# Attention with a product-key expert layer: the filter's statistics, gates and norms reordered against the residual addition

## The reference

```python
xn = layernorm(x)
# attention: 16 heads of 8
q = xn @ Wq + bq;  latent = xn @ Wl + bl            # latent: 32
k = latent @ Wk + bk;  v = latent @ Wv + bv
attn = softmax(q @ k.T * 8 ** -0.5) @ v @ Wo + bo
# expert layer: 8 heads of 32
f = (xn @ fWq + fbq).reshape(B, S, 8, 32)
f = (f - f.mean((0, 1, 2))) / sqrt(f.var((0, 1, 2)) + 1e-5) * gamma + beta   # over all tokens
f0, f1 = l2norm(f[..., :16]), l2norm(f[..., 16:])
s0, s1 = f0 @ l2norm(key0).T, f1 @ l2norm(key1).T    # 32 keys each
# the best 4 of s0 and of s1, softmax over their 16 sums -> weights w of 16 experts
out = x + attn + sum_k w_k * gelu(down[idx_k] . xn) * up[idx_k]
```

## Time and profile before

| | |
|---|---|
| runs | 390.57, 387.48, 390.49 us; median 390.49 |
| profiled execution | 391.01 us, its span 389.2 us |
| TensorE busy | 327.7 us (84%), weight loads 175.9 |
| VectorE busy | 339.8 us (87%) |
| ScalarE busy | 261.1 us (67%) |
| GpSimd busy | 254.7 us (65%) |
| mean granted TensorE clock | 0.956 |
| DMA | 24.81 MB, mean 64 GB/s |

### The profile page before, as it was taken

The page is one execution under the profiler, slowest core; times in us unless marked ns, Lnnn a source line. Parts: engine busy times, 40 slices in busy tenths (PEclk is TensorE's granted clock), DMA queues, the critical chain, the costliest instruction groups (busy, mean ns, idle before and its releaser), DMA issues.

```text
span 389.2 us, 9689 instructions
## 1 busy us (share of the span) xinstructions
PE 327.7 (84%) x3080; PEld 175.9 (45%) x3080; DVE 339.8 (87%) x1409; ACT 261.1 (67%) x412; POOL 254.7 (65%) x544
## 2 busy tenths in 40 slices
PE   3999960878699889898989889898989898898975
PEld 2455540433235445444545445444545454454443
DVE  5699989767977999999999999999999999999571
ACT  4689960697755676676676776666676766767771
POOL 6488899000665676857767676758667677758780
PEclk9999995599659999999999999999999999999999
DMA  5565664000944041231404051432404050000100
GB/s 165 143 185 149 176 179 120 2 1 7 114 49 81 24 62 41 60 77 22 99 2 98 16 84 43 56 70 31 92 7 98 9 92 18 2 17 3 29 15 13
DMA packets 45886, 24.81 MB, mean 64 GB/s; under 512 B 5452, under 2 KB 45708, under 8 KB 45836
## 3 DMA queue, kind: packets, MB, share of 16 engines
q1 hardware_dynamic: 45836, 24.20, 29.1%
HBM read 15.54 MB, written 8.39 MB: 61 GB/s over the span
## 4 chain that ended last, share of the span: by engine, by line
PE 52%; DVE 26%; ACT 11%; issue 7%; POOL 3%; POOLq 0%; ACTq 0%; DVEq 0%
PE bank L605 12%; DVE negm L822 9%; PE bank L634 8%; PE bank L651 8%; PE SI L531 6%; DVE r_sb L886 6%; PE SJ L584 6%; ACT Eb L363 3%; DVE bnv L785 3%; ACT s_sb L380 2%; PE bank L676 2%; PE bank L678 2%; PE bank L677 2%; DVE fst L744 1%; PE SI L456 1%
## 5 line engine op out<-in xcount | busy, mean ns | idle before, releaser
L822 DVE TENSOR_REDUCE negm<-SI 128x4 f32<-128x1024 f32 x128 | 154.8, 1219 | 5.5 <-PE SI L531 5.1
L413 ACT ACTIVATE Eb<-SJ 128x1024 f32<-128x1024 f32 x128 | 130.4, 1019 | 32.1 <-PE SJ L584 31.9
L1039 POOL TENSOR_TENSOR prod<-r_sb,a 128x1024 f32<-128x1024 f32 x31 | 60.2, 1943 | 26.9 <-issue 25.9
L605 PE MATMUL bank<-Eb,vhat 128*18 128x256 f32 x1024 | 70.3, 393 | 0.0
L531 PE MATMUL SI<-KS,QS 48*128 48x256 bf16 x512 | 52.0, 282 | 14.2 <-DVE negm L822 13.9
L584 PE MATMUL SJ<-QS,KS 50*128 50x256 bf16 x512 | 51.7, 282 | 9.0 <-ACT Eb L413 8.8
L866 DVE MAX8 top<-s_sb 128x8 f32<-128x32 f32 x512 | 50.6, 181 | 4.6 <-ACT s_sb L380 4.5
L886 DVE MATCH_REPLACE8 r_sb<-top,s_sb 128x36 f32<-128x36 f32 x256 | 43.1, 181 | 0.0
L531 PEld LDWEIGHTS SI<-KS,QS 48*128 48x128 bf16 x512 | 18.2, 96 | 53.0 <-issue 46.7
L651 PE MATMUL bank<-cst,prod 128*128 128x128 f32 x256 | 34.6, 278 | 4.2 <-ACT s_sb L380 3.7
L634 PE MATMUL bank<-kblk,fqT 128*128 128x256 f32 x128 | 37.1, 413 | 0.5 <-ACT s_sb L380 0.4
(11 more groups left out here) (145 smaller groups left out, 615.9 us busy)
## 6 DMA issues: line engine op xcount, KB each, us to landing
qk_parts<-parts SPq DMA_DIRECT2D x48, 128.0 KB, 2.4
QS<-qk_parts SPq DMA_DIRECT2D x32, 96.0 KB
KS<-qk_parts SPq DMA_DIRECT2D x32, 96.0 KB
x_sb<-L_attn_x SPq DMA_DIRECT2D x8, 256.0 KB, 3.9
QS<-qk_parts SPq DMA_DIRECT2D x32, 64.0 KB
KS<-qk_parts SPq DMA_DIRECT2D x32, 64.0 KB
out<-ysb SPq DMA_DIRECT2D x16, 128.0 KB, 3.1
QS<-qk_parts SPq DMA_DIRECT2D x32, 32.0 KB
```

What stands on the lines that cost most here:

```text
L413: A(Eb[:, n % 4, :], SJ[:, :], ACT.Exp).then_inc(s["ex"], 1)
L605: last = mm(psO[32 * c:32 * c + 2 * VC, (q % 2) * S:(q % 2 + 1) * S], vhat[:, v0:v0 + 2 * VC], Eb[:, (2 * g + c // 2) % 4, e0:e0 + S], sta ...
L822: V.tensor_reduce(negm[:, bb % 2, :, :, pr].rearrange("p t e -> p e t"), SI[slot % 2][:, :].rearrange("p (e t j) -> p e t j", e=2, j=S), a ...
L1039: TT(prod[:, t, :, :, :], r_sb[:, hs, 0:NK].unsqueeze(2).to_broadcast([P, FH, TOP, NK]), a0[:, hs, :].unsqueeze(3).to_broadcast([P, FH, TO ...
```

## The change

- `fbq` is added when ScalarE evacuates the features (`features`), so the addition to the mean (L785), two `bnv` columns and the second offset go. The two `fbq` loads move from the third group of loads to the second (`WLOADS`, semaphore `w`), ahead of six loads of `x`.
- With one offset for both halves, the squares of a chunk are one instruction of 1,024 columns, one chunk a slot in slots 2 to 9, and the scaling in place is one instruction a batch.
- The last chunk's round stands by itself: TensorE makes features, then q and k, then v; ScalarE evacuates the features ahead of the q and k parts; VectorE takes the statistics first and weaves q, k and v between the steps to the scale. ScalarE's second parts of the last chunk come after the first square.
- `downT` is evacuated by ScalarE. In each slot TensorE makes the scores `si` first, then norms, then the gate; gates are in slots 0 to 7, norms in 2 to 9. The key product is in slot 3, its mask on VectorE in slot 4; inverses in slots 4, 6, 8, 10; root in slot 10, transpose and copy in slot 11.
- The residual addition waits for `bn`.

```diff
-        sq = [Eb[:, 1 + i, :].rearrange("p (r n) -> p r n", r=2) for i in range(2)]
+        sq = [Eb[:, 1 - i, :].rearrange("p (r n) -> p r n", r=2) for i in range(2)]
...
-                A(fqT[:, r, c * CH:(c + 1) * CH], psF[i % 3], ACT.Copy).then_inc(s["f_ev"], 1)
+                A(fqT[:, r, c * CH:(c + 1) * CH], psF[i % 3], ACT.Identity, bias=vecs[:, 4 + r:5 + r]).then_inc(s["f_ev"], 1)
...
+            features(NC - 1, 0)
+            features(NC - 1, 1)
+            first_part(NC - 1, 0)
+            first_part(NC - 1, 1)
+            act.wait_ge(s["dT"], 1)
+            A(downT[:, :], psX[1][:, 0:E], ACT.Copy).then_inc(s["downT"], 1)
+            act.wait_ge(s["bc"], 1)
+            A(bnv[:, 6:7], bnv[:, 5:6], ACT.Sqrt).then_inc(s["bd"], 1)
...
+                    A(sq[c % 2], fqT[:, :, c * CH:(c + 1) * CH], ACT.Square,
+                      bias=bnv[:, 8:9], scale=bnv[:, 7:8]).then_inc(s["sq"], 1)
+                    if c == 0:
+                        second_part(NC - 1, 0)
+                        second_part(NC - 1, 1)
...
+            for c in range(NC - 1):
+                project_qk(c)
+                project_f(c)
+                turn_x(c + 1)
+                project_v(c)
+            pe.wait_ge(s["xnT"], NC)
+            project_f(NC - 1)
+            project_qk(NC - 1)
+            project_v(NC - 1)
+            bn_mean()
+            pe.wait_ge(s["w2"], NW2)
+            mm(psX[1][:, 0:E], down_sb[:, :], ident, start=True, stop=True).then_inc(s["dT"], 1)
...
+                if FILTER <= slot < FILTER + NC:
+                    norms(slot - FILTER)
+                c = slot
+                if c < NC:
...
+                    mm(psG[c % 2], downT[:, :], xnT[:, c * CH:(c + 1) * CH], start=True, stop=True).then_inc(s["g"], 1)
+                if slot == 3:
+                    pe.wait_ge(s["krep"], 1)
+                    mm(psM[:, 0:NK], keys_rep[:, :, :, :].rearrange("k h a d -> k (h a d)"), cst[0:NK, 0:NK],
+                       start=True, stop=True).then_inc(s["kmm"], 1)
...
+            feature_moments(NC - 2)
             feature_moments(NC - 1)
+            dve.wait_ge(s["f_st"], 2 * NC)
+            for r in range(2):
+                last = V.bn_aggr(fmv[:, r, :], fst[:, r, :, :])
+            last.then_inc(s["ba"], 1)
+            q_ev(NC - 1)
+            bn_shift()
+            k_ev(NC - 1)
+            bn_deviation()
+            v_rows(NC - 1)
+            bn_scale()
...
-            V.tensor_tensor(bnv[:, 0:2], fmv[:, :, 0], vecs[:, 4:6], ALU.add).then_inc(s["ba"], 1)
...
                     if slot == 4:
-                        pool.wait_ge(s["xn"], NC)
+                        pool.wait_ge(s["bn"], 1)
```

More of the change, by code:

```diff
@@ L332, in _ @@
             deviations(1)
-            for c in range(NC):
-                if c + 1 < NC:
-                    normalise(c + 1)
+            for c in range(NC - 1):
+                normalise(c + 1)
                 first_part(c, 0)
@@ L346, in _ @@
                     A(keys_n[:, :, 1], keys_n[:, :, 0], ACT.Sqrt).then_inc(s["kn3"], 1)
+            features(NC - 1, 0)
[6 more added lines that the diff above has]
+            A(bnv[:, 6:7], bnv[:, 5:6], ACT.Sqrt).then_inc(s["bd"], 1)
             for slot in range(NSLOT):
                 k = slot % 8
[L350 to L365, removed]
                 if FILTER <= slot < FILTER + NC:
                     c = slot - FILTER
+                    if c == 0:
+                        act.wait_ge(s["bn"], 1)
+                        act.wait_ge(s["xT"], NC)
+                    if c >= 2:
+                        act.wait_ge(s["n2"], c - 1)
+                    A(sq[c % 2], fqT[:, :, c * CH:(c + 1) * CH], ACT.Square,
+                      bias=bnv[:, 8:9], scale=bnv[:, 7:8]).then_inc(s["sq"], 1)
+                    if c == 0:
+                        second_part(NC - 1, 0)
+                        second_part(NC - 1, 1)
                     act.wait_ge(s["g"], c + 1)
@@ L420, in _ @@
                 if k == 6 and slot < NPAIR * B:
[L422 to L426, removed]
+                    fb = fqT[:, :, slot // 8 * S:(slot // 8 + 1) * S]
+                    A(fb, fb, ACT.Identity, bias=bnv[:, 8:9], scale=bnv[:, 7:8]).then_inc(s["ff"], 1)
+                if slot == FILTER + NC:
                     act.wait_ge(s["n2r"], NC // 2)
@@ L486, in _ @@
             pe.wait_ge(s["wkv_ev"], 1)
[L487 to L499, removed]
             def bn_mean():
                 pe.wait_ge(s["ba"], 1)
-                pe.wait_ge(s["downT"], 1)
                 for r in range(2):
-                    last = mm(psX[0][:, 0:1], avg, bnv[:, r:r + 1], start=(r == 0), stop=(r == 1))
+                    last = mm(psX[0][:, 0:1], avg, fmv[:, r, 0:1], start=(r == 0), stop=(r == 1))
                 last.then_inc(s["ba"], 1)
@@ L552, in _ @@
                 if slot == 0:
-                    bn_mean()
-                if slot == 1:
                     bn_variance()
[L556 to L564, removed]
+                if slot == FILTER + NC + 1:
                     pe.wait_ge(s["n2s"], 1)
@@ L626, in _ @@
                     t = k - 1
+                    if b == 0 and t == 0:
+                        pe.wait_ge(s["kblk"], 1)
                     if t == 0:
@@ L750, in _, with bn_shift, bn_deviation, bn_scale @@
             scales(1)
-            for c in range(NC):
+            def bn_shift():
+                dve.wait_ge(s["ba"], 2)
+                chain(V.tensor_copy(bnv[:, 4:5], psX[0][:, 0:1]))
+                chain(V.tensor_scalar(bnv[:, 10:12], fmv[:, :, 0], bnv[:, 4:5], None, ALU.subtract))
+                chain(V.tensor_tensor(bnv[:, 12:14], bnv[:, 10:12], bnv[:, 10:12], ALU.mult))
+                V.tensor_tensor(bnv[:, 2:4], bnv[:, 12:14], fmv[:, :, 1], ALU.add).then_inc(s["bb"], 1)
+            def bn_deviation():
+                dve.wait_ge(s["bb"], 2)
+                V.tensor_scalar(bnv[:, 5:6], psX[0][:, 2:3], BN_EPS, None, ALU.add).then_inc(s["bc"], 1)
+            def bn_scale():
+                dve.wait_ge(s["w2"], NW2)
+                V.tensor_scalar(bnv[:, 10:11], bnv[:, 4:5], -1.0, None, ALU.mult)
+                dve.wait_ge(s["bd"], 1)
+                chain(V.reciprocal(bnv[:, 14:15], bnv[:, 6:7]))
+                chain(V.tensor_tensor(bnv[:, 7:8], bnv[:, 14:15], vecs[:, 2:3], ALU.mult))
+                V.tensor_scalar(bnv[:, 8:9], bnv[:, 10:11], bnv[:, 7:8], vecs[:, 3:4], ALU.mult, ALU.add).then_inc(s["bn"], 1)
+            for c in range(NC - 1):
                 if c >= 1:
```

59 lines of the change are left out of this document (18 added, 41 removed).

## The result

The changed kernel takes 374.47 us (median of 4 runs, 373.05 to 377.74) against 390.53 before (4 runs, 387.48 to 390.69): a ratio of 0.962, 95% interval 0.954 to 0.970. The forecast was 381.5, range 374 to 388, with a chance of 0.84 of faster than before. The direction and the places of the gain were right, its size was not: 16 us where 9 were forecast. The profiled execution is the slowest of the four, 377.74 with a span of 375.7, so 13.3 under the profiled one of before.

The account below looks back on a forecast made before the run. VectorE was taken to bound the loop, which would start earlier: 12.3 us gained to the scale, 3.2 lost to the first exponential, small terms +0.2 +0.2 -0.3, sum -9.0. From 391.01 that gave 382.0, set to 381.5; own range 378 to 386.

Parts of the forecast that it names:

- the no-fall rival: Clock does not fall at 59 us; first exponential about 85.1, time 376, or 374 without both stalls; chance 0.22.
- the stalls: Before the solved scale, VectorE's shift and gamma product wait for GpSimd's q and k residues; scale 59.8, 58.1 without both.
- What bounds the kernel: From 130 to 370 us VectorE, busy 94%, sets the loop, whose length stays; the change only starts it earlier.
- Part 1: Up to the solved scale and offset: they come at 59.8 us, 12.3 earlier than 72.15.
- two inputs and a wait for a gap: At L785, 10.63 us: VectorE instructions with both inputs in SBUF wait until GpSimd's run has a gap.
- Part 2: Solved scale to first exponential: TensorE sets the pace; exponential at 90.5, 30.7 us after the scale, 3.2 slower than before.
- The return at about 76, as before: In the filter slots, the clock that falls at about 59 us is back at 76, about 17 us low.
- the sequential tail: After slot 8, from the mT copy to the table load for the exponential, steps in sequence: 7.7 us.
- The second stretch: Low clock stretch at the loop's start, about 17 us, moves along with the first exponential and is left as is.
- bites more: Second low stretch also lies on slots with the turned products; 2 to 6 us given back, 385 to 388; chance 0.12.
- Part 3: Small things: bias at evacuation 0.2 us lost, moved bias loads 0.2 lost, one-instruction filter scaling 0.3 gained.
- The mask beside the residual addition: Residual additions beside slots 2 to 6 hold up VectorE's key mask or reciprocals; 3 us more, 384.5; chance 0.06.

Follow-up runs that it names:

- Experiment 1: The kernel before, with only the residual addition made to wait for the solved scale; 380.48 us.
- kernel 11: The kernel before, with L785 as a one-tensor-input tensor_scalar that adds the first half's bias to both halves; 390.62 us.
- kernels 3, 4, 10, 12, 13: Changed kernel, ScalarE's second parts early: 3 with the wait (376.61 us), 4 without (374.80); 10, 12, 13 add an unread VectorE addition to 4 (378.58, 377.83, 377.07).
- experiment 2: The changed kernel with the residual addition's wait put back to the last chunk's xn; 375.03 us.
- experiments 1 to 8: The follow-up kernels with four runs each, the first made from the kernel before, the others from the changed kernel; 373.59 to 380.48 us.
- kernel 5: The changed kernel with three unread 512-column TensorE products, behind the first scores, the variance product and the first gate; 373.59 us.
- experiments 2 and 4: The changed kernel with the residual addition's wait put back (375.03 us); the same with ScalarE's second parts also right behind the root (374.80 us).
- kernel 6: The changed kernel with unread TensorE products in three gaps ahead of the loop and one in each of slots 11 to 13; 374.14 us.

## Why the prediction was right, and where it was off

The forecast came true in direction, place and range, and was 7.0 us too cautious. The measured 374.5 is also what the no-fall rival gave (376, or 374 without the stalls), but not by its mechanism: the clock did fall at 59, and the stalls came.

- **What bounds the kernel: right.** The loop kept its pace, and 13.5 of the 13.75 us gained by the first exponential reached the end.
- **Part 1: right in size, partly in reason.** Scale at 59.57 (forecast 59.8), both stalls where they were put. Measured from the last L734 it is 14.25 us, where the forecast had 14.9 (59.8 less 44.91): 0.6 better, of which a front 0.4 us later hid the most. Experiment 1 shows that GpSimd's run held L785. But the reason given, two inputs and a wait for a gap, fell: the one-input form is held as long (kernel 11), and a gapless run let eight two-input instructions in at its boundaries (kernels 3, 4, 10, 12, 13). The pair it was read from does not tell the two apart: behind the L925 that ends at 45.21 GpSimd did pause, 0.05 us until 45.26, and L734 got in there. The forecast did not suffer, because both rules give the same end of the two stalls, as the prediction noted.
- **Part 2: mis-sized, and here the difference lies.** "The return at about 76, as before" is the step that failed. It copied the 17 us of before, in which TensorE stood still for the first nine; now it worked from 58.3 on, and the clock was back at 66. All nine profiles of the changed kernel and its variants in which the clock fell here had it low for 7 us, and so had experiment 1, whose only edit takes the standstill away. Both profiles with the standstill (before and kernel 11) have 17. So the standstill is most likely what made it 17. Scores, norms and gate of slots 2 to 5, priced at 3.57 us each, ran at half clock in slot 2 alone: the gates of slots 1 to 4 took 2.07, 1.74, 1.12 and 1.12 us, not 2.0. Slots 2 to 5 with the key product took 10.0 us (63.4 to 73.3) in place of 13.8, which is 3.8 of the difference; 0.6 is in the sequential tail. (The prediction's own terms for the tail and the return at 76 add up to 90.3, not 90.5.) Part 2 took 26.34 us, not 30.7: 4.4 of the 4.5 us by which the span of this execution came out below its forecast. The sign it had named, an exponential at about 90.5, was not there: it came at 85.91.
- **The second stretch** was left as it is. In the profiled execution that was so (17 us, 86.6 to 103.7). The other three runs, 373.05 to 375.00, had a mean clock of 0.982 in place of 0.968, as had experiment 2, whose profile shows 7 us there. Those three have no profile, so that their second stretch was as short is worked out from the mean clock: 14 us low in all, 7 for each stretch. By the slots 12 to 24 above, 7 us in place of 17 are worth 3.6 us, and they run 2.7 to 4.7 below the profiled one. This is the rest of the gap to the median, and the rival "bites more" went the other way. Whether the change has a part in it was not tested. Before, a mean clock as high as one stretch of 17 and one of 7 us give (0.969) came in 2 of the 14 runs beside experiments 1 to 8; now 3 of 4 runs have the short second stretch.
- **Part 3.** The bias at the evacuation costs 0.09 us (0.67 against 0.58 for 512 columns). Five rounds of the front loop, from VectorE's third L734 (17.56 before, 17.64 now) to its last, take 27.67 us in place of 27.35: 0.3 lost, forecast 0.2. The projections start at 10.49 in both kernels, so the moved loads cost nothing that shows there, and the loop kept its length, so the one-instruction scaling gained nothing. In sum some 0.3 us lost where 0.1 was forecast.
- **The rivals.** The fall was avoided only when forced (kernel 5), and was worth 1.6 us, where this rival had 5.4. The mask beside the residual addition took its 0.42 us, as L831 had said.

## What to carry to other kernels

A tiny instruction on the path that lasts ten microseconds and ends with another engine's run is a matter of placing: moving that engine's bulk work behind the point brought 10 of 16 us with one line. In the new order the same line is worth nothing that shows (experiments 2 and 4). Reordering the last chunk kept 1.0 of the 2.5 us that it took, which only undoing it showed, and only when measured from a point that both executions share. And do not copy the length of a low clock stretch to a new schedule: the first was 17 us behind a standstill and 7 without it, the second differs between executions with the same work (17 and 7 us), and that difference was worth more than several of the edits. List the mean clock of each run beside its time when kernels differ by 1% or less.

## What the hardware showed that I had not expected

- A VectorE instruction of two columns was held through two (1.45 us) or six (10.63 us) GpSimd instructions in one place, and eight others, with the same kind of GpSimd work beside them, got in at the end of the one under way.
- The granted clock's low stretches (1.2 GHz) ahead of the loop and at its start were about 7, 10, 14 and 17 us long in these profiles. The profiles of the changed kernel and of experiment 2 have the same TensorE work behind the first exponential, and yet the second stretch is 17 us in one (86.6 to 103.7) and 7 in the other (87.9 to 94.7). So what TensorE does is not all that sets it. Experiment 2:

```profile
88.00:90.00 2.00, 1.31 (x12) 0.65 (x14) 2.00 (x13) 1.02 (x1) 1.72 (x5) 0.50 0.98 105
90.00:96.00 6.00, 4.42 (x42) 1.59 (x40) 5.62 (x27) 4.45 (x5) 5.23 (x16) 0.61 0.88 94
96.00:98.00 2.00, 2.00 (x30) 0.84 (x32) 2.00 (x8) 1.10 (x2) 1.32 (x7) 1.00 0.34 42
```

- A low stretch can also come in the drain and cost there: 31.5 us from the last reduction to the end in kernel 6 and 31.3 in experiment 1, against 29.95 in the kernels without one.
